# Dividing the image half of the attention probabilities on GpSimd instead of ScalarE

## What is computed

```
q = rms_norm(linear(x, q_w, q_b)) ; k, v of ctx[:, 257:] ; k_img, v_img of ctx[:, :257]
img_x = softmax(q @ k_img.T / sqrt(32)) @ v_img          # 16 heads of 32
txt_x = softmax(q @ k.T / sqrt(32)) @ v
x = x + linear(txt_x + img_x, o_w, o_b)                  # x was normalised before q
x = x + sum over the two chosen experts of share * mlp(layernorm(x))
```

## Time and profile before

| | |
|---|---|
| median of 3 runs | 869.69 us (866.67 to 873.19) |
| the profiled execution | 870.31 us |
| its span, first to last instruction | 868.5 us |
| busy: PE / DVE / ACT / POOL | 767.1 / 603.7 / 495.2 / 231.2 us |
| mean granted clock of TensorE | 0.94 of full speed |

### The profile page before, as it was taken

How to read it: one execution, slowest core, us unless ns; L and a number is a source line. 1 busy time by engine, 2 the same in 40 slices (tenths; PEclk the granted TensorE clock), 3 DMA queues, 4 the chain that set the end, 5 groups by cost and what they waited for, 6 DMA issues and landing times.

```text
span 868.5 us, 17362 instructions
## 1 busy us (share of the span) xinstructions
PE 767.1 (88%) x5934; PEld 668.7 (77%) x5934; DVE 603.7 (70%) x1276; ACT 495.2 (57%) x1131; POOL 231.2 (27%) x286
## 2 busy tenths in 40 slices
PE   3879898999999999764299999999999999999991
PEld 2657676767776767543299999999999999999991
DVE  5476878787878787657166768676767767676853
ACT  4366777777777777682044645554555455454640
POOL 3232334343433333104710303021111112030301
PEclk9999999999999999665599999999999999999996
DMA  6631001020202010405845565656665657565663
GB/s 217 251 135 55 22 38 53 39 65 27 66 26 72 20 43 3 180 21 220 300 157 194 212 216 194 255 174 251 212 247 175 250 198 259 179 246 187 222 213 125
DMA packets 28929, 130.68 MB, mean 150 GB/s; under 512 B 4316, under 2 KB 4332, under 8 KB 17872
## 3 DMA queue, kind: packets, MB, share of 16 engines
q1 hardware_dynamic: 23264, 114.26, 37.3%
q0 software_dynamic: 5616, 15.81, 5.1%
HBM read 113.14 MB, written 19.01 MB: 152 GB/s over the span
## 4 chain that ended last, share of the span: by engine, by line
PE 72%; DVE 11%; ACT 7%; issue 5%; DMA 1%; POOL 1%; SPq 0%; ACTq 0%; DVEq 0%; POOLq 0%
PE tiles L1040 7%; PE tiles L1042 7%; PE tiles L1041 7%; PE scores L1304 4%; PE scores L1302 4%; PE scores L1303 4%; PE ptb L1150 4%; PE ptb L1040 3%; PE ptb L1041 3%; PE ptb L1042 3%; PE pvb L1042 3%; PE pvb L1040 3%; PE pvb L1041 3%; PE pvb L1173 2%; PE scores L1140 2%
## 5 line engine op out<-in xcount | busy, mean ns | idle before, releaser
L834 DVE TENSOR_TENSOR w<-scr,w 128x2048 fp32r<-128x2048 f32 x76 | 174.1, 2291 | 69.9 <-ACT w L624 69.9
L624 ACT ACTIVATE w<-scr 128x2048 fp32r<-128x2048 f32 x76 | 144.8, 1907 | 60.7 <-PE scores L1304 59.3
L470 POOL DMA_INDIRECT out_dram<-scr,tok x18 | 36.5, 2030 | 301.1 <-DVE scr L1030 298.4
L606 ACT ACTIVATE scr<-scr,rsum 112x257 f32<-112x257 f32 x128 | 66.4, 519 | 62.8 <-DVE rsum L818 62.7
L1040 PE MATMUL tiles<-c,w 128*128 128x256 f32 (+1 forms) x272 | 81.3, 299 | 18.1 <-DVE c L722 15.5
L1042 PE MATMUL tiles<-w 128*128 128x256 f32 x288 | 81.5, 283 | 0.0
L1041 PE MATMUL tiles<-w 128*128 128x256 f32 x288 | 81.5, 283 | 0.0
L1040 PE MATMUL tiles<-w 128*128 128x256 f32 x288 | 81.5, 283 | 0.0
L1150 PE MATMUL ptb<-ident,scr 112*128 112x112 f32 x384 | 65.2, 282 | 18.3 <-ACT scr L614 16.6
L1042 PE MATMUL tiles<-c,w 128*128 128x256 f32 (+1 forms) x272 | 78.7, 289 | 0.0
L1041 PE MATMUL tiles<-c,w 128*128 128x256 f32 (+1 forms) x272 | 78.7, 289 | 0.0
(11 more groups left out here) (214 smaller groups left out, 2291.4 us busy)
## 6 DMA issues: line engine op xcount, KB each, us to landing
scr<-in_dram SPq DMA_DIRECT2D x86, 1024.0 KB, 4.8
scr<-in_dram SPq DMA_DIRECT2D x8, 750.0 KB, 4.6
scr<-slots_d SPq DMA_DIRECT2D x10, 528.0 KB, 3.7
slots_d<-rows SPq DMA_DIRECT2D x8, 528.0 KB, 11.6
xn<-in_dram SPq DMA_DIRECT2D x10, 256.0 KB, 3.1
xb<-in_dram SPq DMA_DIRECT2D x8, 224.0 KB, 2.9
xr<-in_dram SPq DMA_DIRECT2D x8, 224.0 KB, 2.5
out_dram<-x SPq DMA_DIRECT2D x8, 224.0 KB, 2.8
```

The source lines that it names most:

```text
L606: act.activation(probs[0:L, s, 0:IMG], probs[0:L, s, 0:IMG], ACT.Copy, scale=rsum[0:L, g, s, 0:1]).then_inc(S["normal_img"], 1)
L624: act.activation(EH[slot], raw[slot], ACT.Copy).then_inc(S["eh_done"], 1)
L834: dve.tensor_tensor(EL[slot], raw[slot], EH[slot].bitcast(F32), ALU.subtract).then_inc(S["el_done"], 1)
```

## The change

GpSimd gets a function `divide(b, h)`, which waits for `inverted` and multiplies the image part by its inverse sum with one `tensor_scalar`, in place, and raises `normal_img`. It is called as the first thing in each slot, for the head of the slot before. ScalarE's `normalise` and its calls are gone. The waits of all others stay as they were.

```diff
+            def divide(b, h):
+
+                s, g = h % 4, (h // 4) % 2
+                pool.wait_ge(S["inverted"], NH * b + h + 1)
+                pool.tensor_scalar(probs[0:L, s, 0:IMG], probs[0:L, s, 0:IMG], rsum[0:L, g, s, 0:1], None,
+                                   ALU.mult).then_inc(S["normal_img"], 1)
+
...
                 for h in range(NH):
+                    if h == 0 and has_tail(b):
+                        divide(b - 1, NH - 1)
+                    if h and has_heads(b):
+                        divide(b, h - 1)
...
-            def normalise(b, h):
-                s, g = h % 4, (h // 4) % 2
-                act.wait_ge(S["inverted"], NH * b + h + 1)
-                act.activation(probs[0:L, s, 0:IMG], probs[0:L, s, 0:IMG], ACT.Copy,
-                               scale=rsum[0:L, g, s, 0:1]).then_inc(S["normal_img"], 1)
-
...
-                    if h == 0 and has_tail(b):
-                        normalise(b - 1, NH - 1)
-                    if h and has_heads(b):
-                        normalise(b, h - 1)
```

## The result

The changed kernel takes 904.0 us (median of 4 runs, 901.1 to 905.4) against 870.2 us before in runs beside them: 3.8% slower, ratio 1.038 with a 95% interval of 1.034 to 1.041, or about 33 us. The profiled execution took 903.2 us, span 901.4. The direction was forecast, the size was not: 11 us were forecast.

What follows compares the result with a forecast made beforehand. The prediction took PE's throughput to bound the attention stage. Its terms, 7.8 + 0.55 + 4.5 - 1.6, summed to +11.3 us on the profiled 870.3: 881.6 us, 881.0 in terms of the median; forecast's own range 876 to 887, overall 863 to 892.

Steps and rivals of the forecast that it cites:

- the walk through slots 13 to 0: Work queued behind the waiting division makes L722 and L1040 1.3 us late: 7.8 us over batches 0-5, 0.55 in batch 6.
- What bounds the kernel, and what is removed: Middle batches bound by PE; removing 128 ACT copies is worth at most PE's waits for L614, 16.6 us in all.
- The price of the division: GpSimd multiplication of 112x257 with a pointer scalar, bounded from other rows: 0.50 us taken, 0.38 and 0.73 kept.
- the 0.8 that the prediction named as a sign of being wrong: A division on GpSimd taking over 0.8 us alone would show the forecast wrong.
- The race for the port: After each inverse DVE starts before POOL: L820 keeps 0.28 us, the division ends 0.68 us after the inverse.
- Rival three: POOL wins the port race: L820 takes 0.3 us more per head, 9 to 10 us more, about 890; chance 0.11.
- Slot 1: Back-to-back DVE work shuts POOL out, delaying head 0's transposition by a mean 0.75 us, 4.5 us over batches 1 to 6.
- Slots 3, 7 and 11, squares: L830 waits 0.8 us at these slots, covered by DVE's wait for scores; squares have slack: nothing counted in middle batches.
- Batch 7: Removed copies ahead of the last exponentials win 3.2 us, uncovered slots 7 and 11 lose 1.6: net -1.6 us.
- the 0.61 of batch 7: Mean granted clock past 350 us, where PE is busy 33.9 of 50 and has little to do in batch 7.

Runs made afterwards that it cites:

- e9_tail: The change for heads 13, 14 and 15 alone, ScalarE dividing the other thirteen: 892.9 us, ratio 1.027 to the kernel before.
- e3_queue: Kernel before, ScalarE's copies kept, plus the same waiting GpSimd instruction in each slot on its own buffer, read by nobody: 902.9 us, ratio 1.033.
- e5_cheap: Changed kernel with the division written as a two-input product, the inverse broadcast along the row: 897.1 us, ratio 1.031 to the kernel before.
- e7_both: Changed kernel with the edits of e5_cheap and e6_port together: 894.7 us, ratio 1.029 to the kernel before.
- e13_head13: Only head 13 of each batch divided on GpSimd (pointer form, slot 14), all others on ScalarE: 890.7 us, ratio 1.021 to the kernel before.
- e6_port: Changed kernel with GpSimd's context cast at slot 14 waiting until VectorE has split the keys: 900.7 us, ratio 1.035 to the kernel before.
- e15_head0: Only head 0 of each batch divided on GpSimd (slot 1), all others on ScalarE: 882.3 us, ratio 1.012 to the kernel before.
- e16_squares: Only heads 8, 9 and 10 divided on GpSimd (slots 9, 10 and 11), all others on ScalarE: 877.2 us, ratio 1.006 to the kernel before.
- e14_head14: Only head 14 of each batch divided on GpSimd (slot 15), all others on ScalarE: 880.0 us, ratio 1.007 to the kernel before.
- e8_last: Kernel before with GpSimd dividing in batch 7 alone, in the two-input form: 868.7 us, ratio 0.998 (0.996 to 1.000).

## Why the prediction was wrong in size

The direction and the mechanism held, the queue behind the waiting division; the sum (+11.3 us) was a third of the 33 us. The step that failed is the walk through slots 13 to 0, forecast at 8.35 us and measured at 23 (e9_tail). It had VectorE's L805 take its usual 0.61 us once the queries' cast was there, and L826, for which the gate waits, 0.57 us late. The changed kernel shows 1.88 us for it, as a second GpSimd cast kept the port, and 0.93 instead of 0.50 for the division, and the walk ended without the clock. By its own steps:

- **What bounds the kernel, and what is removed: right.** ScalarE's time is worth nothing in the middle batches; ScalarE waits 161 us for PE in the changed kernel. The relief by itself was not run; e3_queue has 28 of the 33 us without it.
- **The price of the division: wrong, the step where I bounded it.** I took 0.50 us and an upper end of 0.73; it is 0.93 alone, over the 0.8 that the prediction named as a sign of being wrong. I let the number of tensor inputs decide which row was nearest, while the engine's multiplications with a scalar cost more than both kinds of rows I had. By the forecast's own sum it is worth 3 x 0.43 x 6, about 8 us; no run gives it alone, as e5_cheap changes the port as well. (The line through the two casts comes to 0.40 us at 257 columns, not 0.38, which changes nothing here.)
- **The race for the port: right.** VectorE started L821 0.06 us ahead of the division, and L821 stays at 0.28 us in the timeline of the changed kernel above. Rival three (GpSimd first) did not come about in the changed kernel; it did in e5_cheap and e7_both, with the other form of the division.
- **Slots 13 to 0: right place, mis-sized.** 7.8 + 0.55 us against 23 (e9_tail), of which head 13 alone brings 18 (e13_head13). I had VectorE's two subtractions run as soon as their casts were there, with L452 shut out until both were through. Instead GpSimd's next instruction got the port first: L806 took 1.88 us (in e13_head13 it was the second one, 1.38). The third rival gave a price to that order for L820 alone, not for these subtractions. So L826 of before was not 0.57 us late but about 2.3: 0.57, 0.43 for the division and 1.27 for L806 make 2.27, and PE's stand at the gate grew from 0.44 to 2.71 us, by 2.27. e6_port shows that about 1.0 of it hangs on the context's cast. For PE the gate was the place where it hurt, before L722 was ever reached.
- **Slot 1: right place, mis-sized.** 0.75 us a batch predicted, 1.7 measured (e15_head0). The transposition is 1.1 us late, 0.43 of it the price of the division; the rest of the 1.7 fits the clock, which makes the next stretch 0.9 us longer in the mean, less what is caught up later in the batch.
- **Slots 3, 7 and 11, squares: half right.** VectorE's wait for `attended_high` is there, 33.5 us in all with slot 15, and PE loses only 0.4 us between heads 0 and 9 in the changed kernel. The step "squares ... nothing" failed: 0.5 us a batch, 5 us by e16_squares.
- **The clock: absent from the sum.** In the changed kernel the mean granted clock from 90 to 370 us is 0.95, against 0.99 from 90 to 350 us before. At two levels of 0.5 and 1 that is 28 us against 5 at the lower one. An estimate from it: at most half of the 23 us more, about 11 us. The changed kernel itself shows how the two divide around the gate, as the clock fell there less in some batches than in others. From the transposition of head 13 to the next scores, batches 1, 2 and 5 take 7.5 us at 0.64 to 0.69, batches 3 and 4 take 6.2 us at 0.89 and 5.8 us at 0.96; before it is 3.26 us at full clock in four batches of six. So the queue with the longer division costs 2.5 us or more there at nearly full clock, and the clock adds up to 1.8. A low clock is not dear by itself: e14_head14 has the same mean, 0.95, and loses 6 us in all. No experiment here holds the clock fixed.
- **Batch 7: not shown.** -1.6 predicted; -0.9 us from batch 7 on in the changed kernel, one trace against one, and -1.6 us in e8_last, whose interval reaches no change. The sign fits, the size may be luck.

The busy times by stretch behind the point on the clock. Changed kernel: the middle batches, then the stretch from the transposition of head 13 to the next scores in batch 2 and in batch 4:

```profile
90.00:370.00 280.00, 247.88 (x2063) 188.69 (x2067) 211.57 (x594) 146.06 (x545) 194.47 (x240) 0.95 0.12 37
186.23:193.76 7.53, 4.81 (x18) 3.53 (x18) 5.86 (x14) 0.45 (x1) 3.18 (x6) 0.64 0.10 30
282.05:287.82 5.77, 3.05 (x18) 2.09 (x18) 4.14 (x11) 0.45 (x1) 3.15 (x5) 0.96 0.10 21
```

The kernel before, the middle batches and that stretch in batch 4; then e14_head14, the middle batches:

```profile
90.00:350.00 260.00, 241.95 (x2123) 187.21 (x2123) 207.91 (x616) 190.79 (x661) 97.63 (x147) 0.99 0.13 40
258.90:262.16 3.26, 2.82 (x18) 2.07 (x18) 3.19 (x11) 1.99 (x7) 1.47 (x2) 1.00 0.09 17
```

```profile
92.50:357.00 264.50, 247.70 (x2093) 192.66 (x2094) 207.08 (x607) 186.59 (x652) 100.84 (x152) 0.95 0.12 39
```

The Trainium skill, TensorE: Matmul & The Clock Gate, section What's actually happening, has it that the default state is throttled and activity releases the throttle, with nothing between the two levels. These rows agree: PE, busy 46.8 of 50 us in the middle stretch of the earlier trace rows, kept full clock, and the long stands are followed by 0.64 to 0.69 in three batches of five (the gate, changed kernel) and by 0.59 to 0.70 in four of six (slot 2, e15_head0). By the Trainium skill a term for the clock belonged beside the stalls of the forecast; I had used neither it nor the 0.61 of batch 7 for that.

What stays open: why GpSimd's waiting instruction got the port ahead of VectorE in slot 14 and not in slot 1, and why the form of the division decides who is held. That it is so is in the rows; no run here tells the rule. Open is also why the clock fell after the same stall in some batches and not in others, and how the 33 us divide exactly between queue, price and clock.

## What to carry to other kernels

On an in-order engine a new instruction that waits costs what is queued behind it, even if nobody needs its result: 28 of 33 us came without a reader, and 20 of these 28 went with the wait. Before work is moved to an idle engine, look at the place of its wait in that engine's list and who waits for the next entries; idle share says nothing about that. A cheaper form of an instruction is to be judged in place and not alone: 0.32 us less on GpSimd came with 0.45 us more on VectorE beside it. And where the bound engine is TensorE, allow after each stall of some microseconds for what the lower clock can cost.

## What the runs showed of the hardware

- GpSimd on 112x257 fp32, alone: copy 0.40 us, product with a broadcast second tensor 0.61, product of two tensors 0.73, `tensor_scalar` with an immediate 0.86, with a pointer 0.93. `tensor_scalar` on 118 columns takes 0.59, so 2.4 ns a column; the two-input forms are cheaper.
- A GpSimd instruction that comes up behind back-to-back VectorE work waits for all of it (2.24 us for 0.93), while two GpSimd casts in a row held one VectorE subtraction (1.88 us for 0.61, and 0.89 with the second cast kept back).
- A VectorE `tensor_scalar` on 112x118 that starts 0.06 us ahead of GpSimd's `tensor_scalar` takes 0.28 us; 0.04 us ahead of GpSimd's product with a broadcast second tensor it takes 0.73 us. Whether the form or the start decides isn't shown.
- The same 34 TensorE instructions took 2.7 us at a granted clock of 1.00 or 4.2 us at 0.59, after the same stall of 1.76 us.
